# A two-layer kernel whose instruction order comes from a planner: the planner's durations, handoffs, one modelled conflict and its offsets are replaced

## The reference, cut to what matters

```python
xn = layernorm(x)
x = x + mamba(xn) + experts(xn)         # layer 0
xn = layernorm(x)
x = x + sphere_attn(xn) + window_net(xn)   # layer 1

# mamba: 256 inner channels, 16 states, a scan over 256 tokens
h = exp(dt * A) * h + dt * B * xs;   y = sum_n(h * C) + D * xs;   out = (y * silu(z)) @ W
# experts: 8 experts, each token goes to one of them
out = where(chosen == e, (relu(x @ w1[e] + b1[e]) @ w2[e] + b2[e]) * prob, 0)
# sphere_attn: 16 heads of 8; the score is a power of 1 + the arc between q and k,
# divided by row and column sums
s = (1 + arccos(clip(q . k))) ** -3.2
# window_net: 2 layers of 8-head attention (head size 64) over windows of 64 with
# normalised q and k and a rotary term, then a gated gelu network of 341 channels
```

## Time and profile before

| | us |
|---|---|
| median of 3 runs | 2417.98 |
| lowest and highest run | 2406.57, 2421.41 |
| profiled execution: span from first to last instruction | 2423.0 |
| TensorE busy in it | 1912.3 (79%) |
| VectorE busy | 1905.3 (79%) |
| ScalarE busy | 1819.8 (75%) |
| GpSimd busy | 611.8 (25%) |

### The profile page before, as it was taken

The page is one execution under the profiler, slowest core; times in us unless marked ns, Lnnn a source line. Parts: engine busy times, 40 slices in busy tenths (PEclk is TensorE's granted clock), DMA queues, the critical chain, the costliest instruction groups (busy, mean ns, idle before and its releaser), DMA issues.

```text
span 2423.0 us, 31144 instructions
## 1 busy us (share of the span) xinstructions
PE 1912.3 (79%) x10610; PEld 1286.1 (53%) x10610; DVE 1905.3 (79%) x2685; ACT 1819.8 (75%) x2507; POOL 611.8 (25%) x270
## 2 busy tenths in 40 slices
PE   3767788898777888887787888878778787888776
PEld 2533446675545555554555555545445555556555
DVE  5878885538998799869997998878986988765563
ACT  2435778888768888787778887788778687888884
POOL 2532211222222213212232222322222222213220
PEclk9887879998879789888888888989898988997887
DMA  7731205531110120011101110101101110000000
GB/s 242 240 106 58 70 18 146 148 88 62 44 44 9 49 75 27 9 50 53 48 5 41 40 56 18 45 11 47 40 23 41 42 55 18 1 1 5 1 1 5
DMA packets 67517, 126.19 MB, mean 52 GB/s; under 512 B 8836, under 2 KB 40132, under 8 KB 67236
## 3 DMA queue, kind: packets, MB, share of 16 engines
q1 hardware_dynamic: 61808, 113.19, 14.7%
q0 software_dynamic: 2816, 7.21, 0.9%
q10 hardware_dynamic: 2740, 3.80, 0.4%
HBM read 111.33 MB, written 12.85 MB: 51 GB/s over the span
## 4 chain that ended last, share of the span: by engine, by line
PE 29%; DVE 29%; issue 20%; ACT 18%; DMA 2%; SPq 1%; DVEq 0%; ACTq 0%; another core or an unknown queue 0%
PE ps L776 6%; DVE hB L1458 6%; PE ps L968 5%; DVE hB L1464 3%; PE ps L1010 3%; DVE hB L1452 3%; PE ps L1070 3%; ACT L771 3%; ACT arena L1281 2%; ACT arena L1289 2%; DVE arena L1529 2%; DVE n_c L1537 2%; DVE lss L1583 2%; ACT arena L1355 2%; DVE rb L1590 2%
## 5 line engine op out<-in xcount | busy, mean ns | idle before, releaser
L1749 POOL TENSOR_TENSOR arena<-arena 128x1024 f32<-128x1024 f32 x128 | 359.2, 2826 | 972.5 <-ACT arena L1283 972.5
L776 PE MATMUL ps<-w_ident,arena 128*128 128x128 f32 x1647 | 276.6, 316 | 135.6 <-ACT arena L1355 42.8
L968 PE MATMUL ps<-hB,w_ident 128*128 128x512 f32 x512 | 305.6, 728 | 70.7 <-DVE hB L1464 68.8
L776 PEld LDWEIGHTS ps<-w_ident,arena 128*128 128x128 f32 x1647 | 223.8, 164 | 228.3 <-issue 113.6
L1458 DVE TENSOR_TENSOR_SCAN hB<-dA,hB 128x1024 f32<-128x1024 f32 x128 | 321.1, 2514 | 1.0 <-ACT dA L1245 0.6
L1753 POOL TENSOR_TENSOR arena<-arena,rb 128x1024 f32<-128x1024 f32 x64 | 159.2, 2487 | 622.5 <-DVE rb L1590 622.5
L1070 PE MATMUL ps<-w_l_wqkv,arena 128*128 128x512 f32 x384 | 205.3, 666 | 30.7 <-DVE rb L1590 12.5
L1245 ACT ACTIVATE dA<-mv,w_A_log 128x510 f32<-128x510 f32 x256 | 168.3, 714 | 70.9 <-DVE hB L1458 68.0
L1452 DVE TENSOR_TENSOR hB<-BC,mv 128x1024 f32<-128x1024 f32 x128 | 194.3, 1522 | 29.8 <-PE ps L968 28.1
L1529 DVE TENSOR_SCALAR arena<-ps 128x1024 f32<-128x1024 f32 x128 | 155.8, 1217 | 58.9 <-PE ps L1010 54.6
L1355 ACT ACTIVATE arena<-ps,nmx 128x128 f32<-128x128 f32 (+1 forms) x512 | 159.2, 394 | 55.6 <-DVE nmx L1610 52.7
(11 more groups left out here) (210 smaller groups left out, 4066.0 us busy)
## 6 DMA issues: line engine op xcount, KB each, us to landing
BC<-bc_d SPq DMA_DIRECT2D x128, 512.0 KB
BC<-in_experts SPq DMA_DIRECT2D x16, 514.0 KB
arena<-in_experts SPq DMA_DIRECT2D x15, 514.0 KB
mv<-in_experts SPq DMA_DIRECT2D x15, 514.0 KB, 3.4
arena<-in_x SPq DMA_DIRECT2D x8, 256.0 KB, 5.5
xnT_d<-arena SPq DMA_DIRECT2D x8, 256.0 KB, 10.9
hB<-xnT_d SPq DMA_DIRECT2D x8, 256.0 KB
x<-in_x SPq DMA_DIRECT2D x8, 256.0 KB, 2.8
```

What stands on the lines that cost most here:

```text
L776: return t.transpose(out_, in_, ident[0:k, 0:k])
L968: e = t.matmul(lb(), ident, hB[k % 2][:, j], start=q == 0 and j == 0, stop=q == NQ - 1 and j == NG - 1)
L1749: g.tensor_tensor(la[m % 2][:, half], la[m % 2][:, half], cl[:, half], ALU.subtract).then_inc(g_sub, 1)
```

## The change

Nothing changes in what is computed, in the instructions, in the semaphores or in the buffers. The planner's inputs and rules change, and with them the order of each engine's list and the PSUM banks:

- the durations in `STAGES` and `stages()`;
- the handoffs: `LANDS` now has a value for each engine, and `lands()` applies them;
- a table load counts 1.29 us in place of 1.3 and `SWITCH` is 80 in place of 62;
- a rule: when a unit of `DUAL` starts on VectorE while one of `POOLED` runs on GpSimd, its planned duration grows by what is left of that one, and the other way round;
- the offsets `LATER` and `STREAM`; `STREAM` has entries for more streams (experts, loads, `f_`, `o`, `z`).

```diff
--- before.py
+++ after.py
@@ -56,45 +56,59 @@
 
 
 STAGES = {
-    "e_ln": [("DVE", 1.7), ("ACT", 0.6)], "e_xn": [("DVE", 0.7)], "e_tr": [("PE", 0.6), ("ACT", 0.5), ("SP", 0.1)],
-    "e_lg": [("PE", 0.6)], "e_route": [("DVE", 1.0), ("ACT", 0.5)], "e_pre": [("PE", 0.4)], "e_place": [("DVE", 5.0)],
-    "e_load": [("SP", 0.6)], "e_xt": [("PE", 0.15), ("ACT", 0.35)], "e_up": [("PE", 1.1), ("ACT", 1.2)],
-    "e_down": [("PE", 1.7), ("DVE", 0.3)], "e_store": [("SP", 0.1)],
-    "m_weights": [("ACT", 0.4), ("DVE", 0.2)], "l_weights": [("DVE", 3.0)], "m_load": [("SP", 0.1)], "m_xp": [("PE", 2.4), ("ACT", 0.5), ("SP", 0.1)],
-    "m_dt": [("PE", 1.15), ("ACT", 2.3)], "m_du": [("DVE", 1.3)], "m_B": [("SP", 0.1)], "m_C": [("SP", 0.1)],
-    "m_ex": [("ACT", 1.25)], "m_bx": [("DVE", 1.35)], "m_scan": [("DVE", 2.4)], "m_hc": [("DVE", 1.35)], "m_sum": [("PE", 2.3)],
-    "m_fin": [("DVE", 1.5)], "x_load": [("SP", 0.1)], "m_out": [("PE", 2.1), ("DVE", 0.62)],
-    "f_yg": [("POOL", 4.0)], "f_ln": [("DVE", 2.9), ("ACT", 0.6)], "f_xn": [("DVE", 1.1)], "f_tr": [("PE", 0.6), ("DVE", 0.7)],
-    "g_qkv": [("PE", 0.86), ("DVE", 0.5)], "g_sq": [("ACT", 1.05), ("DVE", 1.5)], "g_norm": [("ACT", 0.7)],
-    "g_hd": [("DVE", 0.4), ("PE", 0.6), ("ACT", 0.5)], "g_score": [("PE", 1.3), ("DVE", 1.2)], "g_ln": [("ACT", 3.9)],
-    "g_sub": [("POOL", 2.4)], "g_tan": [("ACT", 3.8)], "g_pow": [("ACT", 3.9)], "g_av": [("DVE", 2.9), ("PE", 1.1)],
-    "g_ev": [("ACT", 0.5)], "g_avT": [("PE", 0.6), ("DVE", 1.15)], "g_oT": [("PE", 0.6), ("ACT", 0.5)],
-    "g_out": [("PE", 1.2), ("DVE", 0.65)], "out": [("DVE", 0.65), ("SP", 0.1)], "zeros": [("DVE", 0.3)],
-    "shift": [("PE", 0.4), ("ACT", 0.8)], "norm": [("DVE", 0.2), ("ACT", 0.5)], "qn": [("DVE", 1.25)], "heads": [("PE", 1.2), ("ACT", 0.9)],
-    "score": [("PE", 1.4), ("DVE", 0.85), ("ACT", 1.3)], "pt": [("PE", 0.9), ("ACT", 0.7)], "pv": [("PE", 0.85)], "on": [("DVE", 0.7)],
-    "oT": [("PE", 0.6), ("ACT", 0.5)], "wo": [("PE", 2.3), ("DVE", 0.4)], "ln": [("PE", 0.8), ("DVE", 0.8), ("ACT", 0.5)],
-    "ln2": [("DVE", 0.65)], "lnT": [("PE", 0.35), ("DVE", 0.45)], "up": [("PE", 1.25)], "gelu": [("ACT", 1.15)],
-    "hid": [("DVE", 0.42)], "down": [("PE", 1.8), ("DVE", 0.4)],
+    "e_ln": [("DVE", 1.28), ("ACT", 0.55)], "e_xn": [("DVE", 1.11)], "e_tr": [("PE", 0.44), ("ACT", 0.6), ("SP", 0.1)],
+    "e_lg": [("PE", 1.1)], "e_route": [("DVE", 2.0), ("ACT", 0.3)], "e_pre": [("PE", 0.35)], "e_place": [("DVE", 4.6)],
+    "e_load": [("SP", 0.6)], "e_xt": [("PE", 0.11), ("ACT", 0.3)], "e_up": [("PE", 0.89), ("ACT", 1.15)],
+    "e_down": [("PE", 0.89), ("DVE", 0.3)], "e_store": [("SP", 0.1)],
+    "m_weights": [("ACT", 0.4), ("DVE", 0.2)], "l_weights": [("DVE", 1.4)], "m_load": [("SP", 0.1)], "m_xp": [("PE", 1.72), ("ACT", 0.6), ("SP", 0.1)],
+    "m_dt": [("PE", 0.95), ("ACT", 2.7)], "m_du": [("DVE", 1.42)], "m_B": [("SP", 0.1)], "m_C": [("SP", 0.1)],
+    "m_ex": [("ACT", 1.34)], "m_bx": [("DVE", 1.22)], "m_scan": [("DVE", 2.28)], "m_hc": [("DVE", 1.22)], "m_sum": [("PE", 1.72)],
+    "m_fin": [("DVE", 1.47)], "x_load": [("SP", 0.1)], "m_out": [("PE", 1.8), ("DVE", 0.69)],
+    "f_yg": [("POOL", 4.8)], "f_ln": [("DVE", 2.46), ("ACT", 0.55)], "f_xn": [("DVE", 1.11)], "f_tr": [("PE", 0.44), ("DVE", 0.68)],
+    "g_qkv": [("PE", 0.65), ("DVE", 0.62)], "g_sq": [("ACT", 1.06), ("DVE", 1.54)], "g_norm": [("ACT", 0.9)],
+    "g_hd": [("DVE", 0.29), ("PE", 0.44), ("ACT", 0.59)], "g_score": [("PE", 1.06), ("DVE", 1.22)], "g_ln": [("ACT", 4.05)],
+    "g_sub": [("POOL", 2.36)], "g_tan": [("ACT", 3.86)], "g_pow": [("ACT", 3.95)], "g_av": [("DVE", 2.84), ("PE", 1.0)],
+    "g_ev": [("ACT", 0.6)], "g_avT": [("PE", 0.44), ("DVE", 1.05)], "g_oT": [("PE", 0.44), ("ACT", 0.6)],
+    "g_out": [("PE", 0.89), ("DVE", 0.68)], "out": [("DVE", 0.69), ("SP", 0.1)], "zeros": [("DVE", 0.34)],
+    "shift": [("PE", 0.22), ("ACT", 0.97)], "norm": [("DVE", 0.17), ("ACT", 0.5)], "qn": [("DVE", 1.22)], "heads": [("PE", 0.88), ("ACT", 1.03)],
+    "score": [("PE", 1.11), ("DVE", 0.88), ("ACT", 1.25)], "pt": [("PE", 0.66), ("ACT", 0.81)], "pv": [("PE", 0.64)], "on": [("DVE", 0.78)],
+    "oT": [("PE", 0.44), ("ACT", 0.6)], "wo": [("PE", 1.83), ("DVE", 0.42)], "ln": [("PE", 0.69), ("DVE", 0.77), ("ACT", 0.54)],
+    "ln2": [("DVE", 0.72)], "lnT": [("PE", 0.22), ("DVE", 0.54)], "up": [("PE", 0.86)], "gelu": [("ACT", 1.2)],
+    "hid": [("DVE", 0.48)], "down": [("PE", 1.34), ("DVE", 0.42)],
 }
 
-LANDS = {"SP": 4.5, "POOL": 2.0}
+LANDS = {"PE": 0.27, "ACT": 0.12, "DVE": 0.12, "SP": 4.5, "POOL": 0.15}
+LOAD_TIME = 1.29
+
+DUAL = ("m_du", "m_bx", "m_scan", "m_hc", "m_fin", "qn", "g_hd")
+POOLED = ("g_sub", "qkv")
 
 NEEDS = {"e_ln": "ln", "e_route": "ln", "m_weights": "ln", "m_dt": "ln", "m_ex": "ln", "f_ln": "ln", "g_norm": "ln", "g_ln": "ln", "g_pow": "ln",
          "norm": "ln", "score": "ln", "ln": "ln", "m_in": "silu", "g_tan": "tan", "gelu": "gelu"}
-SWITCH = 62.0
-
-LATER = {"down": 7, "e_down": 10, "e_lg": -58, "e_ln": 10, "e_load": -157, "e_place": -21, "e_pre": -90, "e_route": -51,
-         "e_scat": -16, "e_store": -20, "e_tr": 2, "e_up": 2, "e_xn": -13, "f_ln": 82, "f_tr": -44, "f_xn": 51, "f_yg": -57,
-         "g_av": 29, "g_avT": -106, "g_ev": -197, "g_hd": -39, "g_ln": 56, "g_norm": -70, "g_oT": 58, "g_out": 9, "g_pow": 46,
-         "g_qkv": -51, "g_score": 2, "g_sq": -6, "g_sub": -109, "g_tan": 35, "gelu": -26, "heads": 23, "hid": -10,
-         "l_weights": 6, "ln": 1, "ln2": 28, "lnT": -1, "m_B": 58, "m_C": 123, "m_bx": -13, "m_dt": 19, "m_du": -143,
-         "m_ex": -25, "m_fin": 51, "m_hc": 6, "m_in": -1, "m_load": 77, "m_out": -190, "m_scan": 33, "m_sum": 2,
-         "m_weights": -18, "m_xp": 25, "norm": 8, "oT": -14, "on": -2, "pt": -18, "pv": 51, "qn": -17, "score": 9,
-         "shift": 28, "up": -19, "wo": 59, "x_load": -158, "zeros": -12}
-
-STREAM = {("g", 0): -3, ("g", 3): -3, ("g", 4): -6, ("g", 5): -29, ("g", 6): 1, ("g", 7): -23, ("l", 0): 1, ("l", 2): -2,
-          ("l", 3): 9, ("l", 4): -5, ("l", 5): -3, ("l", 6): 19, ("l", 7): -4, ("m", 0): -5, ("m", 1): 6, ("m", 2): 34,
-          ("m", 3): 23, ("m", 4): -11, ("m", 5): 1, ("m", 6): 8, ("m", 7): 12}
+SWITCH = 80.0
+
+LATER = {"down": 14, "e_down": 23, "e_lg": 147, "e_ln": 161, "e_load": -254, "e_place": -20, "e_pre": -161, "e_route": -498,
+         "e_scat": 136, "e_store": -224, "e_tr": 83, "e_up": 3, "e_xn": -139, "e_xt": -1, "f_ln": 169, "f_tr": -247, "f_xn":
+         338, "f_yg": 163, "g_av": 43, "g_avT": -159, "g_ev": -426, "g_hd": -41, "g_ln": 68, "g_norm": -536, "g_oT": 57,
+         "g_out": 8, "g_pow": 60, "g_qkv": -315, "g_score": 0, "g_sq": -1, "g_sub": -153, "g_tan": 39, "gelu": -46, "heads":
+         22, "hid": -29, "l_weights": -29, "ln": -7, "ln2": 26, "lnT": 5, "m_B": 3, "m_C": 539, "m_bx": -14, "m_dt": 16,
+         "m_du": -305, "m_ex": -27, "m_fin": 139, "m_hc": 7, "m_in": -2, "m_load": 151, "m_out": -452, "m_scan": 35, "m_sum":
+         35, "m_weights": 114, "m_xp": -62, "norm": 4, "oT": -152, "on": -4, "out": -115, "pt": -17, "pv": 49, "qkv": 0, "qn":
+         -8, "score": 9, "shift": 29, "up": -10, "wo": 61, "x_load": 30, "zeros": -64}
+
+STREAM = {("e", 0): 12, ("e", 1): 5, ("e", 2): 9, ("e", 3): 23, ("e", 4): -45, ("e", 5): 11, ("e", 6): -56, ("e", 7): 12,
...
+          ("f", 4): -58, ("f", 5): -47, ("f", 6): -15, ("f", 7): -6, ("g", 0): -2, ("g", 1): 1, ("g", 2): 0,
+          ("g", 3): -10, ("g", 4): -7, ("g", 5): -27, ("g", 6): 2, ("g", 7): -21, ("l", 0): 1, ("l", 1): 1, ("l", 2): -8,
+          ("l", 3): 10, ("l", 4): -10, ("l", 5): -2, ("l", 6): 21, ("l", 7): 0, ("m", 0): -21, ("m", 1): 4, ("m", 2): 33,
+          ("m", 3): 22, ("m", 4): -3, ("m", 5): 20, ("m", 6): -1, ("m", 7): 37, ("o", 0): -33, ("o", 1): 59, ("o", 2): 37,
...
 
 LOADED = [15.0, 24.0]
 
@@ -110,12 +124,16 @@
 def stages(unit):
     u, n, b, k = unit
     if u == "m_in":
-        return [("PE", 1.1), ("ACT", 0.6)] if k % 2 else [("PE", 1.1), ("DVE", 2.9), ("ACT", 0.65)]
+        return [("PE", 0.86), ("ACT", 0.62)] if k % 2 else [("PE", 0.86), ("DVE", 3.15), ("ACT", 0.62)]
     if u == "e_scat":
-        return [("POOL", 1.3 * TT * (GP[n + 1] - GP[n]))]
+        return [("POOL", 1.5 * TT * (GP[n + 1] - GP[n]))]
     if u == "qkv":
-        return [("PE", 1.15), ("ACT", 0.5)] if k % 3 else [("PE", 2.3), ("ACT", 0.95), ("DVE", 3.55), ("POOL", 2.4)]
+        return [("PE", 0.86), ("ACT", 0.6)] if k % 3 else [("PE", 1.72), ("ACT", 1.02), ("DVE", 3.6), ("POOL", 2.36)]
     return STAGES[u]
+
+
+def lands(unit, engine):
+    return 2.0 if engine == "POOL" and unit[0] in ("e_scat", "f_yg") else LANDS[engine]
 
 
 def stream(unit):
@@ -372,6 +390,7 @@
     idle, banks = list(range(8)), {}
     taken = set()
     table = "ln"
+    dual_until = pool_until = 0.0
     events, waiting = [], []
 
 
@@ -452,13 +471,18 @@
                         idle.remove(z)
                 takes = stages(unit)[stage][1]
                 if best[2] and best[2] != table:
```

(11 more changed lines are left out.)

## The result

The change makes the kernel 0.5% faster: the median of 20 runs is 2405.12 us beside 2414.75 for the kernel before, ratio 0.9947 (95% interval 0.9921 to 0.9973). I had forecast 2366, over 2% faster. The profiled execution of the changed kernel, with a span of 2393.8 us, lies at the fast end of its runs (2386.34 to 2424.53), so the two profiles differ by 29 us where the medians differ by 10.

The account below looks back on a forecast made before the run. Taken as bound by four interlocking in-order lists, the kernel was to gain 16 + 4 + 27 + 5 = 52 us, from 2423 to 2371 profiled, 2366 in the median; 8-in-10 range 2298 to 2450.

Parts of the forecast that it names:

- What bounds the kernel: Whole kernel: no engine is a wall; four in-order lists interlock, and the lost time is dozens of short waits.
- Durations: Planner's prices: new ones are of operations alone, TensorE's sum off by -20%, ScalarE's by +6%; given no credit.
- Turn-taking: VectorE meeting GpSimd in mamba lines: a third of 112 us saved, at 0.41 each 16 us gained, bounds -23 and +46.
- Table loads: ScalarE's 146 table loads: fewer with the higher SWITCH, each counting 0.39; 4 us gained, bounds -7 and +15.
- Waits in the middle: VectorE's 189 us idle between 700 and 2070 us: a seventh gained, 27 us, bounds a loss of 38 and gain of 75.
- the three terms: The forecast gains for the middle's waits (27 us), table loads (4 us) and start and end (5 us).
- Start and end: Moved last mamba stream and m_sum push VectorE's work towards an end with idle time; 5 us gained, bounds -10 and +20.
- B: Rival: no measurable change, the new lists as good as the old in another arrangement; 2410 us, chance 0.23.
- C: Rival: slower, TensorE's work priced too low, so waits for ps grow and VectorE's share falls; 2443 us, chance 0.24.

Follow-up runs that it names:

- e11: Changed kernel with offsets searched anew from its own, TensorE's prices times 1.2 and ScalarE's and VectorE's overlaps corrected; 0.9796 of the kernel before.
- e15: Changed kernel, offsets searched from its own with another seed, TensorE's prices times 1.2 and overlaps corrected; 2364.34 us, 0.9773 of the kernel before.
- e18: Changed kernel, offsets searched anew, TensorE's prices times 1.15, overlaps corrected, two more units taking turns with GpSimd; 0.9791 of the kernel before.
- e5: Kernel before (old lists) with most arithmetic of GpSimd's subtraction and addition left out, so it hardly meets VectorE; 0.9572 of the kernel before.
- e6: Changed kernel (new lists) with most arithmetic of GpSimd's subtraction and addition left out; 0.9658 of the kernel before.
- e3: Kernel before (old lists) with every TensorE transpose done twice, so more TensorE work; 1.0290 of the kernel before.
- e4: Changed kernel (new lists) with every TensorE transpose done twice; 1.0191 of the kernel before.
- e16: Changed kernel, offsets searched from its own with TensorE's prices times 1.2 as the only correction; 0.9966 of the kernel before.
- e13: Changed kernel with 6 entries of LATER and 12 of STREAM moved by 1 or 2 us at random; 1.0159 of the kernel before.
- e14: Changed kernel with another 18 offset entries moved by 1 or 2 us; 1.0170 of the kernel before.

## Why the prediction was wrong

**What bounds the kernel** was right: four lists that interlock, no wall, many short waits. So were the numbers of operations, and that no cost is added.

**Durations.** I wrote that the new prices are those of an operation by itself, too low for TensorE and too high for ScalarE, and gave them "no credit". In the trace VectorE's and ScalarE's units do have their new prices as medians, nearly all within 0.02 us (`pt` 0.81, `m_ex` 1.33, `g_ln` 4.04), and still e11, e15 and e18 show that correcting the two errors I named is worth 1.5 to 1.7%. So errors that I named and priced at nothing bend the order that a search finds. With the lists held, the change's own prices see a gain of 164 us in the new lists, and the corrected ones 41. Whether the new durations are worse than the old ones no run shows, since no search by the old ones was made. I had the sums and used them for a rival only.

**Turn-taking.** I took 16 us and had it right in kind. The three lines fell by 41 us, more than the third of 112 that I assumed (37), but with the other lines that meet GpSimd VectorE lost only 28 of 158.5 us of meetings (e5, e6). The whole of GpSimd's work is worth 0.65 of a microsecond for each of these 158.5, above my 0.41, its own time included. By that rate the 28 are worth 18 us, by the split of e5 and e6 33. Between these the runs don't decide, and both are inside my bounds.

**Table loads** were right by size: 7 fewer, 9 us of ScalarE's time, at my 0.39 some 3.5 us against 4. No run tests it alone.

**The step that failed is "Waits in the middle"**: I took a seventh of VectorE's idle time there as a gain, 27 us, by judgement. There was no gain. Between the same two scans VectorE's idle time rose from 185 to 199 us, and over the whole span its waits for TensorE grew by 76 us while those for ScalarE shrank by 62. In all its idle time stayed (517.7 and 515.4 us), and e6 beside e5 shows the order as a whole, tables and ends included, to be 0.9% worse, about 21 us on the wrong side, inside the bound of -38 that I gave for the middle and far from the 36 us that I took for the three terms (27, 4 and 5). My sign for the middle compared unlike stretches: VectorE's share between the first and the last scan was 83.4% before and not the 86% of the stage from 700 us, and it is 82.9% now. "Start and end" did not fail by these rows: up to the last scan of pair 2 the changed kernel is 20 us ahead and behind the last scan 5, in two executions that differ by 29. The forecast was 52 us; the ratio gives 13, 33 less 21 by the split above. The granted clock, 0.853 in the profile for 0.862, may have taken a little of it; no run separates that.

**The rivals.** What happened is B in size (0.5%, and I had put the bound between it and a gain at 1%), but not by two equal arrangements: a worse order stands against fewer meetings (e5, e6). C named its signs, the waits for `ps` and a lower share of VectorE, and the trace has them. Its price, that the loss grows with TensorE's slowness, fell in e3 and e4, and e16 shows that TensorE's price by itself is not the whole of it. That both corrections are needed together rests on the searches and the table of prices; one search for each single correction is few, with lists that differ by 2% when offsets move by 2 us. How the overlaps act stays open. The range, 2298 to 2450, held the time.

## What to carry to other kernels

When a planner's prices are replaced by durations from a trace, the sum per engine has to be laid beside the engine's busy time as well: a median duration of an operation by itself is not what it holds the engine for, neither where operations overlap nor where the clock changes. Play the old lists by the new prices as well, before two plans' ends are compared: 64 us in two currencies were 164 in one, and 41 by the prices that fit the chip best. Split a planned gain by its causes before believing it; here one cause gave some 33 us and another took 21, and the sum hid both. And a searched order is one draw among many: moving 18 of its offsets by 1 or 2 us changed the chip's time by 2% (e13, e14).

## What the runs showed of the hardware

Taking work off TensorE, 330 us at the full clock by my estimate, gave only 0.8% under the old lists, and the granted clock fell from 0.862 to 0.741; an estimated 240 us more work raised it to 0.898. TensorE was four fifths busy before, and with less work it got slower matmuls: its busy time fell by 171 us only.

VectorE and GpSimd took turns by whole operations, whatever the size of the one that waits: in the changed kernel an operation of 128x32 elements on VectorE (`g_av`, line 1567, two operands in SBUF) has a median of 191 ns and a maximum of 2380, about one whole GpSimd operation. In e6, with GpSimd's operations cut short, its maximum is 194. It is not so for every operation: the one of line 1553, which has a single operand and reads PSUM, never took more than 1226 ns in the same execution. The rows, of the changed kernel, e6, and the changed kernel:

```profile
L1567 DVE TENSOR_TENSOR vt<-gv,vt x128: 178/191/2380, 263.3 to 2337.3; 128x32 f32<-128x32 f32 x128
```

```profile
L1567 DVE TENSOR_TENSOR vt<-gv,vt x128: 182/190/194, 268.3 to 2275.7; 128x32 f32<-128x32 f32 x128
```

```profile
L1553 DVE TENSOR_SCALAR arena<-ps x128: 1190/1220/1226, 200.0 to 2299.5; 128x1024 f32<-128x1024 f32 x128
```
